# Two constant matmuls into the claimed PSUM tile ahead of the input wait in the small TensorE steps of a two-layer network

## What is computed

```python
# layer 0 mixer: 8 heads of 32
q, k, v, g = x @ w_q + b_q, x @ w_k + b_k, x @ w_v + b_v, x @ w_g + b_g
q, k = _theta_shift(q, sin, cos), _theta_shift(k, sin, cos)
sim = jnp.einsum('bhnd,bhsd->bhns', q, k / scale) * mask[None]     # decay mask
ret = jnp.einsum('bhns,bhsd->bhnd', sim, v)
# per-head normalization, then
return (jax.nn.silu(g) * ret) @ w_o + b_o
# layer 0 feed-forward, weights quantized to -1, 0, 1
hidden = jax.nn.sigmoid(x @ q(w1).T) * (x @ q(w2).T); return hidden @ q(w3).T
# layer 1: causal softmax attention, 16 heads of 16, then 8 experts (top 2) plus a shared expert
x = _layernorm(x + block(x))        # around each of the four blocks
```

## Time and profile before

| | us |
|---|---|
| median of 3 runs | 491.55 |
| lowest and highest | 486.73, 492.25 |
| span of the profiled execution | 489.6 |
| PE busy, share of the span | 405.2, 83% |
| PEld busy | 250.6, 51% |
| DVE busy | 314.7, 64% |
| ACT busy | 196.4, 40% |
| POOL busy | 141.8, 29% |
| mean granted TensorE clock | 0.897 of full |

### The profile page before, as it was taken

One profiled execution on the slowest core, in us unless ns is written; L12 is line 12 of the kernel. 1 busy time (PEld: TensorE's weight loads), 2 busy tenths in 40 slices (PEclk: granted clock), 3 DMA queues, 4 the chain that ended last, 5 costly groups with the idle time before them and its releaser, 6 DMA issues. The chain is left out here.

```text
span 489.6 us, 7799 instructions
## 1 busy us (share of the span) xinstructions
PE 405.2 (83%) x2978; PEld 250.6 (51%) x2978; DVE 314.7 (64%) x689; ACT 196.4 (40%) x356; POOL 141.8 (29%) x182
## 2 busy tenths in 40 slices
PE   2697959568867876888889779998998989999996
PEld 0345646454634542323337334465565757767775
DVE  4547674794877679248438984445646887586554
ACT  4339543123323440588475114635534331241220
POOL 4458874843863000266320001212111000000000
PEclk9879578766989997699899757999999999999999
DMA  7912120200000000005000000000000000000000
GB/s 244 376 28 76 45 55 34 86 0 1 1 1 0 1 2 0 1 11 184 1 0 1 2 0 1 0 3 0 2 2 1 0 1 23 1 0 13 12 12 32
DMA packets 6856, 15.38 MB, mean 31 GB/s; under 512 B 610, under 2 KB 4002, under 8 KB 6818
## 3 DMA queue, kind: packets, MB, share of 16 engines
q1 hardware_dynamic: 6820, 14.89, 9.4%
HBM read 13.84 MB, written 1.05 MB: 30 GB/s over the span
## 5 line engine op out<-in xcount | busy, mean ns | idle before, releaser
L583 PE MATMUL psum_a<-cut_weights,x_transposed 128*128 128x352 f16 (+2 forms) x768 | 141.3, 338 | 12.9 <-DVE cut_weights L1001 8.7
L583 PEld LDWEIGHTS psum_a<-cut_weights,x_transposed 128*128 128x128 f16 x768 | 74.8, 101 | 69.5 <-issue 14.8
L1269 POOL TENSOR_TENSOR ln_rstd<-ln_var_eps,minus_half 128x1 f32<-128x1 f32 x32 | 23.7, 742 | 188.3 <-DVE ln_var_eps L992 188.3
L1286 POOL TENSOR_SCALAR_AFFINE_SELECT arena_mixers<-arena_mixers 128x256 f32<-128x256 f32 (+1 forms) x48 | 24.7, 517 | 108.6 <-ACT arena_mixers L936 108.6
L951 ACT ACTIVATE arena_ffn<-psum_a 128x352 f32<-128x352 f32 x48 | 22.3, 464 | 72.4 <-PE psum_a L583 72.4
L1145 DVE TENSOR_REDUCE arena_mixers<-psum_a 128x2 f16<-128x768 f32 (+3 forms) x44 | 47.3, 1124 | 1.4 <-PE psum_a L740 1.4
L936 ACT ACTIVATE arena_mixers<-psum_a 128x1024 f32<-128x1024 f32 (+2 forms) x48 | 42.0, 883 | 11.1 <-PE psum_a L756 5.7
L1184 DVE SCALAR_TENSOR_TENSOR arena_ffn<-arena_ffn,psum_a 128x352 f32<-128x352 f32 x48 | 24.9, 519 | 31.5 <-ACT arena_ffn L951 16.5
L583 PE MATMUL psum_b<-cut_weights,arena_ffn 128*128 128x256 f16 (+1 forms) x357 | 40.8, 273 | 0.0
L583 PEld LDWEIGHTS psum_b<-cut_weights,arena_ffn 128*128 128x128 f16 (+1 forms) x357 | 34.2, 98 | 5.9 <-issue 1.7
L1187 DVE SCALAR_TENSOR_TENSOR arena_ffn<-arena_ffn,router,psum_a 128x176 f32<-128x176 f32 (+1 forms) x80 | 31.9, 432 | 1.7
(11 more groups left out here) (159 smaller groups left out, 687.0 us busy)
## 6 DMA issues: line engine op xcount, KB each, us to landing
stage<-in_wup SPq DMA_DIRECT2D x8, 512.0 KB, 3.5
stage<-in_wdown SPq DMA_DIRECT2D x4, 512.0 KB, 4.6
arena_ffn<-in_w SPq DMA_DIRECT2D x1, 1408.0 KB, 10.4
stage<-in_xT SPq DMA_DIRECT2D x2, 512.0 KB, 4.4
stage<-in_wqkvg SPq DMA_DIRECT2D x2, 512.0 KB, 5.2
residual<-in_x SPq DMA_DIRECT2D x2, 512.0 KB, 9.1
out<-residual SPq DMA_DIRECT2D x8, 128.0 KB, 1.7
stage<-in_wqkv SPq DMA_DIRECT2D x2, 384.0 KB, 9.9
```

The lines of the kernel that those rows point to most:

```text
L583: ins = mm(dst, lhs[k][a], rhs(k, b, col), start=(k == 0 and a == 0 and b == 0), stop=(bias_at is None and k == n - 1 and a == 1))
L1269: g_.tensor_tensor(rstd[:, r:r + 1], veps[:, r:r + 1], half[:, 0:1], ALU.pow).then_inc(ln_rstd[layer], 1)
L1286: g_.affine_select(out=part, in_=part, compare_op=ALU.is_ge, fill=0.0, base=0, pattern=[[0, se_heads(j)], [1, P]], channel_multiplier=-1). ...
```

## The change

`claim(step)` is called for every step before its input waits, not after them. For the kinds in WARMED (`tqk`, `sc`, `kv`, `ret`, and of `ty`, `wo`, `tx` those of layers 0 and 1) TensorE then issues two matmuls before it waits for the step's input: 256 columns of constants against the identity, into the first 256 columns of the claimed tile. The step's own first matmul, which starts a new accumulation, overwrites them.

```diff
+WARM, WARMED = 2, ('tqk', 'sc', 'kv', 'ret', 'ty', 'wo', 'tx')
...
+            def warm(ps):
+
+                dst = ps if len(ps.shape) == 2 else ps[:, 0, :]
+                for _ in range(WARM):
+                    mm(dst[:, 0:2 * P], ident16, con16[:, 0:2 * P], start=True, stop=True)
+
             for step in SCHEDULE:
                 kind = step[0]
                 if kind not in RING_OF:
                     continue
                 ps = psum(step)
+                claim(step)
+                if kind in WARMED and (kind not in ("ty", "wo", "tx") or step[1] < 2) and step != ("proj", 0):
+                    warm(ps)
...
                 elif kind == "tqk":
                     t = step[1]
                     pe.wait_ge(rotated, t + 1)
-                    claim(step)
```

More of the change, by code:

```diff
@@ L762, in _ @@
                         pe.wait_ge(v_init, 1)
-                    if j == 0:
-                        claim(step)
                     for s in range(4):
```

2 lines of the change are left out of this document (removed).

## The result

The changed kernel takes 496.64 us (median of 4 runs, 493.89 to 497.83), the kernel before 491.9 beside it. The ratio is 1.011 with a 95% interval of 1.007 to 1.015: a little slower, within the 2%. The profiled execution has a span of 496.0 us, against 489.6.

A forecast was written before the change was run, and what follows sets the result against it. Early, PE at half clock (57 us) alternates with DVE, ACT and POOL; PE never stops in the last third. Terms +1.5, -2.4, -0.7, +2.8, -0.9, +0.9, -0.5, +0.4 sum to +1.1 us: 492.5 us, range 481 to 500.

The forecast's parts named there:

- The moved claim "costs nothing of its own": Every step: claiming before the input waits leaves the same waits ahead of the same step, so it adds nothing.
- tx of layer 1 and behind it: After 142.6 us: a few uncovered pairs among DVE-bound row maxima, +0.4 us; behind that the change adds nothing.
- To 50 us, +1.5: Start to 50 us: half clock stays, uncovered pairs delay ACT, bounds 0 and 2.0, taken as +1.5 us.
- 50 to 62 us, -2.4: From 54.65 to 61.78 us: clock holds, so tqk, sc and proj take 4.74 us, not 7.13: -2.4 us.
- 62 to 92 us, -0.7: Ty and ret pairs +0.2, proj half saved -0.9 by a later clock fall; pairs from 80 us hidden behind POOL, 0.
- 92 to 108 us, +2.8: Clock stays at half; six uncovered pairs at 0.43 us and one at 0.22 give +2.8 us.
- 108.5 to 118.7 us, -0.9: First up at half clock is 1.7 us too long; the fall may only be put off, so half: -0.9 us.
- every pair is on the path: Rival, claim comes last: all 70 pairs uncovered, at least 15.4 us, 507 us; chance 0.05.
- the clock does not follow: Rival: pairs do not keep the clock up, terms sum to +6.8, 498.4 us; chance 0.14.
- The later low stretch: Rival, half clock from 275.8 to 299.7 us moves: 5 us either way, 487.5 or 497.5; chance 0.13.
- The clock staying up nearly everywhere: Rival: pairs also fill gaps between steps and keep the clock up, sum -10.2, 481.4 us; chance 0.18.
- The page's rule: Whole kernel: ramp penalty under 1% of the span, so at most 4.9 us to win; the trace was said to disagree.

The follow-up runs named there:

- the 18 pairs: Pairs only in the 18 steps that had a PE wait of 0.47 us or more, claims moved, against the kernel before: 1.0044, 493.04 us.
- the filled kernel: Kernel before, no pairs, with 3 to 44 constant matmuls filling some 80% of the wait in the 36 steps with the longest waits: 0.9637, 472.89 us.
- the claims-only kernel: Claims moved ahead of the input waits, no pair at all, against the kernel before: 1.0052, 494.47 us.

## Why the prediction was right in its range, and where its steps failed

The time lies in the range (481 to 500) and on the side of the sum, 4 us above the 492.5. Neither says much. The range also holds the kernel before (491.9), and the +1.1 of the sum is small beside the errors of its terms. The side was right by luck: what made the kernel slower beyond doubt is the moved claim, which the sum had at nothing. With the claims of the steps without a pair put back, the 70 pairs are not measurably slower (0.9982 to 1.0047). Step by step:

**The moved claim "costs nothing of its own".** This step failed, and it is the one that decides the sign. The same waits stand ahead of the same step, but in another order. The claims alone cost 0.5% (0.2 to 0.8), and with the claims of the other steps put back the 70 pairs take 0.15% more than the kernel before, no difference: 4.7 us less than the change, by the two ratios. The "tx of layer 1 and behind it", +0.4 in the sum, was +3.2 in the trace and -0.2 with the claims put back; this part has few pairs, and its qk, tm and tx of layer 2 start 0.09 us later after each wait, 1.8 us in sum behind 150 us.

**To 50 us, +1.5:** measured +0.4 at ret of tile 1. ACT's step of the earlier trace rows came at 41.35 us, 1.0 late and not 2.0, and PE's wait of 2.33 us ahead of ty took most of the rest (0.99 is left of it in the changed kernel).

**50 to 62 us, -2.4:** -0.2. The clock did hold at 50.5, but fell at 56.9, with proj beginning; 3.3 us at half gave back most of the gain (proj's twelve products took 4.25 us, against 2.77 at full clock). DVE's rotation ahead of the tqk also came 1.0 us later. The 7 pairs of the piece alone were worth nothing in the time, and in their trace the clock was at half from 48.1 to 61.6 us. That these pairs hold the clock there was the assumption of the term; the trace of the change has it so and this one does not.

**62 to 92 us, -0.7:** -0.2. The fall moved from 67.5 to 70.5 and the return stayed, so proj took 4.34 us, 0.4 less than before.

**92 to 108 us, +2.8:** +1.3 in the trace, +1.6 in the kernel with that piece alone. The prices were right (0.43 a pair at half clock), but the clock came back at 104.7 for the last pairs, and some of ret's delay was in DVE's slack.

**108.5 to 118.7 us, -0.9:** +1.6. The wrong sign. The fall was put off by 3 us, but so was the return; the low stretch kept its 10.2 us, and pairs in it cost 0.43 and more. That "putting off" a fall wins half of the stretch was an assumption; here it only moved it.

**118 to 135, +0.9:** +1.0. **139 to 142, -0.5:** -0.7.

**Rivals.** That every pair is on the path is refuted by the 18 pairs that cost nothing beside the claims. That the clock does not follow is refuted by the kernel with pairs of 32 rows in all kinds but sc, which took 504.4 us against 496.6. The later low stretch came ten us later and was 20.4 us long instead of 23.9, but the shift over it only went from +5.2 (250 us) to +6.1 (312.69 us); the expert part behind it kept its length within 0.3 us, as foretold. The clock staying up nearly everywhere was right as a mechanism, but not for this change: pairs do not do it, fills do. The waits that I called unfillable by a pair (5.38 us ahead of ty) were filled by 44 matmuls. Its gain was also sized too low, 10 us, where the fills won 13.2 up to the first dn; and it left out what lies behind 150 us, where 41 us at half were worth another 6.6.

**The page's rule.** The Trainium skill (TensorE: Matmul & The Clock Gate, Part 1: The HAM clock gate) says that for modelling the ramp penalty is less than 1% of a typical kernel's span. The estimate from that page, at most 4.9 us to win, took its figure for a bound on all that the clock can cost. The trace does not agree with such a bound: the filled kernel won 3.6% (17.9 us), with the clock at full where it had been at half for 99 us in ten stretches. What a single ramp costs, which is what the page's figure is about, no run here shows.

## What to carry to other kernels

Where a profile shows TensorE's clock at half in a stretch that waits on PE in turn with other engines, fill its waits with dense matmuls of constants, as many as most of the wait in the trace holds, and put none where PE does not wait. Two matmuls everywhere cost about what they keep of the clock. A fill that is sized for the full clock takes twice as long when the clock is at half and then overruns its wait, so look at the clock of the filled kernel as well. When a semaphore wait is moved past another one, look at the time from the producer's end to the consumer's start before and after: an order of waits that is the same on paper can differ by 0.09 us per step.

## What was not expected of the hardware

- After an input wait that is written first and sits on the weight load, PE started 0.055 us after the producer's end; with the claim written first and the input's wait as an instruction of its own, 0.146 us (medians of tqk, ty, tx and wo in the kernel before and in the claims-only kernel).
- PE busy for 13.96 of 14 us, with 44 matmuls of 32 rows among its work, did not keep the clock; with 44 of 128 rows in their place it stayed at full, at the same 0.11 us a matmul.
- A fall of the clock that came later moved the return as well: 108.5 to 118.7 us became 111.5 to 121.7 (one trace of each kernel).
- The place of a fall moved without any added matmul: at half from 50.5 to 60.7 us in the kernel before, from 39.7 to 46.5 and 56.8 to 60.2 with nothing but the claims moved.
- The cost of pairs is not additive: nine of them alone cost 1.3%, the 70 together, without the moved claims, nothing that can be measured.
